# First product of the gated feed-forward in the second phase: second contraction chunk as bare integers, its scale in the silu, one bf16 term fewer

## The reference, cut to what matters

```
w1 = (fc1_q - 128) * fc1_scales[group of 128 rows]    # [256, 1024], two groups
w2 = (fc2_q - 128) * fc2_scales[group]                # [1024, 256]
h  = layernorm(x) * ln_gamma + ln_beta
y  = silu(h @ w1 + fc1_bias)
z  = y @ w2 + fc2_bias
out = x + tanh(g) * (x + 0.5 * z)                     # per token
```

## Time and profile before

| | |
|---|---|
| median of three executions | 1620.32 us (1616.96 to 1621.4) |
| span of the profiled execution, first to last instruction | 1614.4 us |
| median less that span | 5.9 us |
| PE busy in the span | 1486.5 us (92%) |
| DVE, ACT, POOL busy | 1316.4, 1135.2, 1034.7 us |
| second phase | from 611 us on |

### The profile page before, as it was taken

How to read it: one execution, slowest core, us unless ns; L and a number is a source line. 1 busy time by engine, 2 the same in 40 slices (tenths; PEclk the granted TensorE clock), 3 DMA queues, 4 the chain that set the end, 5 groups by cost and what they waited for, 6 DMA issues and landing times.

```text
span 1614.4 us, 42641 instructions
## 1 busy us (share of the span) xinstructions
PE 1486.5 (92%) x14155; PEld 1144.6 (71%) x14155; DVE 1316.4 (82%) x3187; ACT 1135.2 (70%) x2057; POOL 1034.7 (64%) x1392
## 2 busy tenths in 40 slices
PE   4999999999999972668999999999999999999997
PEld 2788888888888861435667676777777776777666
DVE  4698888888888875778988889898988889898742
ACT  7798888888888742355666666666666666676664
POOL 4588888888888744224556565665656566565445
PEclk9999999999999995588999999999999999999999
DMA  7322222322222002332223232232223232232200
GB/s 228 96 80 66 91 72 65 96 66 69 93 65 71 2 1 92 80 119 73 80 80 87 73 85 80 85 87 81 83 78 92 72 91 74 86 85 84 64 16 22
DMA packets 197690, 125.45 MB, mean 78 GB/s; under 512 B 44400, under 2 KB 196848, under 8 KB 197360
## 3 DMA queue, kind: packets, MB, share of 16 engines
q1 hardware_dynamic: 197616, 124.48, 26.2%
HBM read 92.69 MB, written 25.17 MB: 73 GB/s over the span
## 4 chain that ended last, share of the span: by engine, by line
PE 48%; SPq 4%; DVE 3%; issue 2%; DMA 2%; POOL 2%; ACT 1%; POOLq 0%
PE b_bank L1835 28%; PE b_bank L1910 7%; PE b_scoreT L1892 4%; PE b_score L1875 4%; PE b_bank L1843 2%; PE b_bank L1987 1%; SPq L1306 1%; DMA b_nmT<-b_nm 1%; DMA b_yT<-b_y 1%; SPq L1290 1%; DVE b_nm L1653 1%; SPq L1279 1%; PE b_bank L1925 1%; ACT b_E L1471 1%; SPq L1315 0%
## 5 line engine op out<-in xcount | busy, mean ns | idle before, releaser
L1471 ACT ACTIVATE b_E<-b_scoreT 128x1024 f32<-128x1024 f32 x256 | 262.2, 1024 | 152.5 <-PE b_scoreT L1892 151.3
L1653 DVE TENSOR_REDUCE b_nm<-b_score 128x4 bf16<-128x1024 f32 x256 | 313.3, 1224 | 54.6 <-PE b_score L1875 48.4
L31 ACT ACT_TABLE_LOAD x157 | 201.4, 1283 | 18.6 <-PEq L1059 15.2
L1835 PE MATMUL b_bank<-f,b_YT 128*128 128x256 bf16 x1536 | 190.3, 274 | 4.7 <-POOL b_YT L1404 4.6
L890 PE MATMUL bank<-hT,W1T 128*128 128x256 bf16 x1536 | 183.3, 273 | 2.4 <-DVE hT L706 1.7
L1835 PE MATMUL b_bank<-b_hT,f 128*128 128x256 bf16 x1536 | 183.4, 273 | 0.8 <-DVE X L1749 0.8
L890 PE MATMUL bank<-W2T,G 128*128 128x256 bf16 x1024 | 171.0, 272 | 6.7 <-DVE GT L780 6.2
L1835 PEld LDWEIGHTS b_bank<-f,b_YT 128*128 128x128 bf16 x1536 | 143.5, 98 | 39.7 <-issue 19.5
L1835 PEld LDWEIGHTS b_bank<-b_hT,f 128*128 128x128 bf16 x1536 | 147.7, 98 | 30.3 <-issue 12.6
L890 PEld LDWEIGHTS bank<-hT,W1T 128*128 128x128 bf16 x1536 | 148.0, 98 | 27.7 <-ACT G L549 4.0
L1388 POOL TENSOR_TENSOR b_v<-b_v,b_e 128x512 f32<-128x512 f32 x32 | 40.6, 1269 | 195.0 <-DVE b_e L1734 195.0
(11 more groups left out here) (222 smaller groups left out, 3524.8 us busy)
## 6 DMA issues: line engine op xcount, KB each, us to landing
b_Q<-q_dram SPq DMA_DIRECT2D x192, 64.0 KB, 2.6
b_K<-k_dram SPq DMA_DIRECT2D x192, 64.0 KB, 2.8
xin<-in_x SPq DMA_DIRECT2D x32, 256.0 KB, 3.2
ctxn<-in_ctx SPq DMA_DIRECT2D x32, 256.0 KB, 2.8
mask_in<-in_mask SPq DMA_DIRECT2D x32, 256.0 KB, 3.0
X<-in_x SPq DMA_DIRECT2D x32, 256.0 KB, 4.0
ctxt<-in_ctxT SPq DMA_DIRECT2D x32, 256.0 KB, 4.2
b_ctxt<-in_ctxT SPq DMA_DIRECT2D x32, 256.0 KB, 2.8
```

Source lines behind the costliest of these rows:

```text
L31: act.add_instruction(mybir.InstLoadActFuncSet(name=nc.get_next_instruction_name(), act_func_set_id=which, ins=[], outs=[]))
L1471: nc.scalar.activation(E[:, pair:pair + 2], scoreT_ps[:, :, :, :], ACT.Exp).then_inc(sig["E"], 1)
L1653: nc.vector.tensor_reduce(pair, score_ps[:, :, :, :], AX.X, ALU.max, negate=True).then_inc(sig["nm"], 1)
L1835: last = nc.tensor.matmul(out_tile, lhs(i, k), rhs(j, k), start=start and k == chunks[0] and (i, j) == TERMS[0], stop=stop and k == chunks ...
```

## The change

The second chunk of fc1 (input rows 128 to 255) is kept as the bare integers fc1_q - 128, which bf16 holds without a remainder, so the part (1, 0) of that chunk is all zero and its matmul is left out. The first chunk is scaled by s0 / s1 instead of s0, and the silu multiplies its input by s1, a [128, 1] operand per slice. gamma of the second chunk moves from the weights to hT, so mlp_high and mlp_low are two instructions each, one per chunk. The bias from beta is multiplied by s1 too. A test in the first phase finds out whether the integers and scales allow this; its result joins the mask flag, and the branch that PE takes then (`mask` true) keeps all three terms. The ratio s0 / s1 is computed in the first phase on DVE, written to DRAM and read back as a broadcast row.

```diff
@@ first phase, SP @@
+                                                          ("b1_raw", "fc1_bias_col"), ("s0_col", "fc1_s0_col"),
+                                                          ("s1_col", "fc1_s1_col"))]
+            + [(q1[:, :], a["fc1_q"][P:2 * P])]
...
+                if at_iteration(half, parity, NB):
+                    sp.wait_ge(sig["ratio"], 6)
+                    for i, src in enumerate((second["s0_col"], keep_s)):
+                        sp.dma_start(second["ratio"][i:i + 1].rearrange("o (h p) -> p (o h)", p=P), src[:, :],
+                                     allow_slow_non_contiguous=True).then_inc(sig["ratio_out"], 16)
+                if at_iteration(half, parity, NB + LAGS):
+                    sp.wait_ge(sig["ratio_out"], 32)
@@ first phase, DVE @@
+                if at_iteration(half, parity, 7):
+                    scale, first = second["s1_col"], second["s0_col"]
+                    nc.vector.tensor_tensor(zero_s[:, :], scale[:, :], scale[:, :], ALU.mult).then_inc(sig["square"], 1)
...
+                    nc.vector.tensor_tensor(first[:, :], first[:, :], inv_s[:, :], ALU.mult).then_inc(sig["ratio"], 1)
+                if at_iteration(half, parity, NB + 2):
+                    nc.vector.tensor_scalar(q1[:, :].bitcast(F32), q1[:, :], -128.0, None, ALU.add).then_inc(sig["exact"], 1)
+                    dve.wait_ge(sig["exact"], 1)
+                    nc.vector.tensor_reduce(second["exact"][:, 1:2], q1[:, :].bitcast(F32), AX.X, ALU.max,
+                                            apply_absolute_value=True).then_inc(sig["exact"], 1)
...
@@ setup_b, DVE @@
+            exact = second["exact"]
+            step(V_.tensor_tensor(exact[:, 0:1], exact[:, 0:1], exact[:, 1:2], ALU.min))
+            V_.tensor_tensor(peak[:, 1:2], peak[:, 1:2], exact[:, 0:1], ALU.min)
@@ phase_b, ACT @@
-                    nc.scalar.activation(hT[:, 0], whole_bank(BANK["hT"]), ACT.Copy).then_inc(sig["hhi"], 1)
+                    nc.scalar.activation(hT[:, 0, 0], bank[BANK["hT"]][:, 0], ACT.Copy)
+                    nc.scalar.activation(hT[:, 0, 1], bank[BANK["hT"]][:, 1], ACT.Copy,
+                                         scale=second["g_col"][:, 1:2]).then_inc(sig["hhi"], 1)
...
                         last = nc.scalar.activation(Y[:, 2 * j + i], bank[BANK[f"H{j}"]][:, i], ACT.Silu,
-                                                    bias=b1f[:, 2 * j + i:2 * j + i + 1])
+                                                    bias=b1f[:, 2 * j + i:2 * j + i + 1],
+                                                    scale=second["s1_col"][:, 2 * j + i:2 * j + i + 1])
@@ phase_b, DVE @@
-                    nc.vector.tensor_tensor(hT[:, 1], whole_bank(BANK["hT"]), hT[:, 0], ALU.subtract).then_inc(sig["hlo"], 1)
+                    nc.vector.tensor_tensor(hT[:, 1, 0], bank[BANK["hT"]][:, 0], hT[:, 0, 0], ALU.subtract)
+                    nc.vector.scalar_tensor_tensor(hT[:, 1, 1], bank[BANK["hT"]][:, 1], second["g_col"][:, 1:2], hT[:, 0, 1],
+                                                   ALU.mult, ALU.subtract).then_inc(sig["hlo"], 1)
@@ phase_b, PE @@
-            def product(out_tile, lhs, rhs, chunks, start=True, stop=True):
+            def product(out_tile, lhs, rhs, chunks, start=True, stop=True, last_terms=TERMS):
                 for k in chunks:
-                    for i, j in TERMS:
+                    terms = last_terms if k == chunks[-1] else TERMS
+                    for i, j in terms:
...
                         last = product(bank[BANK[f"H{j}"]][:, i], lambda s, k: f1[:, s, k, c * P:(c + 1) * P],
-                                       lambda s, k: hT[:, s, k], range(C))
+                                       lambda s, k: hT[:, s, k], range(C), last_terms=TERMS if mask else TERMS[:2])
```

More of the change, by code:

```diff
@@ L130, in build @@
             g_col=sb("g_col1", [P, C], F32), b_col=sb("b_col1", [P, C], F32), b1_raw=sb("b1_raw1", [P, HC], F32),
-            ones=sb("ones_row", [1, P], F32))
+            ones=sb("ones_row", [1, P], F32), s0_col=sb("s0_col", [P, HC], F32), s1_col=sb("s1_col", [P, HC], F32),
+            exact=sb("exact", [P, 2], F32),
+            ratio=nc.dram_tensor("ratio", (2, HID), F32, kind="Internal").ap())
         late = whole.enter_context(ExitStack())
@@ L846, in iteration @@
                         [P, C, P])).then_inc(sig["bv_rep"], 1)
+                if at_iteration(half, parity, 7):
+                    scale, first = second["s1_col"], second["s0_col"]
+                    nc.vector.tensor_tensor(zero_s[:, :], scale[:, :], scale[:, :], ALU.mult).then_inc(sig["square"], 1)
+                    dve.wait_ge(sig["square"], 1)
+                    nc.vector.tensor_scalar(zero_s[:, :], zero_s[:, :], 1e-36, None, ALU.is_le).then_inc(sig["ratio"], 1)
+                    dve.wait_ge(sig["ratio"], 1)
+                    nc.vector.tensor_scalar(keep_s[:, :], zero_s[:, :], -1.0, 1.0, ALU.mult, ALU.add).then_inc(sig["ratio"], 1)
+                    dve.wait_ge(sig["ratio"], 2)
+                    nc.vector.tensor_reduce(second["exact"][:, 0:1], keep_s[:, :], AX.X, ALU.min)
+                    nc.vector.tensor_tensor(inv_s[:, :], scale[:, :], zero_s[:, :], ALU.mult)
+                    nc.vector.tensor_tensor(scale[:, :], scale[:, :], keep_s[:, :], ALU.mult).then_inc(sig["ratio"], 1)
+                    dve.wait_ge(sig["ratio"], 3)
+                    nc.vector.tensor_tensor(keep_s[:, :], inv_s[:, :], keep_s[:, :], ALU.add)
+                    nc.vector.tensor_tensor(scale[:, :], scale[:, :], zero_s[:, :], ALU.add).then_inc(sig["ratio"], 1)
+                    dve.wait_ge(sig["ratio"], 4)
+                    nc.vector.reciprocal(inv_s[:, :], scale[:, :]).then_inc(sig["ratio"], 1)
+                    dve.wait_ge(sig["ratio"], 5)
+                    nc.vector.tensor_tensor(first[:, :], first[:, :], inv_s[:, :], ALU.mult).then_inc(sig["ratio"], 1)
[4 more added lines that the diff above has]
+                                            apply_absolute_value=True).then_inc(sig["exact"], 1)
+                    dve.wait_ge(sig["exact"], 2)
+                    nc.vector.tensor_scalar(second["exact"][:, 1:2], second["exact"][:, 1:2], 256.0, None,
+                                            ALU.is_le).then_inc(sig["exact"], 1)
                 for k in range(2):
@@ L1090, in _ @@
             step(V_.tensor_reduce(peak_all[:, 1:2], rows_ps[0:1, 1, 0:P], AX.X, ALU.min))
-            step(V_.tensor_scalar(any_masked[:, :], peak_all[:, 1:2], 0.0, None, ALU.is_equal))
+            step(V_.tensor_scalar(general[:, :], peak_all[:, 1:2], 0.0, None, ALU.is_equal))
             dve.wait_ge(s_pe, 2)
@@ L1237, in _ @@
         def _(sp):
+            ratio_row = second["ratio"].rearrange("(o g) h -> o (g h)", o=1)
             def load_weights(ints, layout, rows, scales, step):
@@ L1575, in iteration @@
                         last = nc.scalar.activation(f1[:, 0, c], whole_YT[:, c * HID:(c + 1) * HID], ACT.Copy,
-                                                    scale=second["g_col"][:, c:c + 1])
+                                                    scale=second["g_col"][:, c:c + 1] if c == 0 else 1.0)
                     last.then_inc(sig["f1hi"], 1)
@@ L1756, in iteration @@
                     dve.wait_ge(sig["b1_mm"], 1)
-                    nc.vector.tensor_tensor(b1f[:, :], second["b1_raw"][:, :], b1_ps, ALU.add).then_inc(sig["b1f"], 1)
+                    nc.vector.tensor_tensor(b1f[:, :], second["s1_col"][:, :], b1_ps, ALU.mult).then_inc(sig["b1s"], 1)
+                    dve.wait_ge(sig["b1s"], 1)
+                    nc.vector.tensor_tensor(b1f[:, :], b1f[:, :], second["b1_raw"][:, :], ALU.add).then_inc(sig["b1f"], 1)
                 if h:
@@ L1817, in iteration @@
                         last = nc.vector.scalar_tensor_tensor(f1[:, 1, c], whole_YT[:, c * HID:(c + 1) * HID],
-                                                              second["g_col"][:, c:c + 1], f1[:, 0, c], ALU.mult,
-                                                              ALU.subtract)
+                                                              second["g_col"][:, c:c + 1] if c == 0 else 1.0,
+                                                              f1[:, 0, c], ALU.mult, ALU.subtract)
                     last.then_inc(sig["f1lo"], 1)
@@ L2073, in iteration @@
                     first_bias()
-            some = pe.value_load(any_masked[0:1, 0:1], min_val=0, max_val=1)
+            some = pe.value_load(general[0:1, 0:1], min_val=0, max_val=1)
             with pe.If(some < 1):
```

26 lines of the change are left out of this document (16 added, 10 removed).

## The result

The changed kernel takes 1689.48 us (median of 4 runs, 1688.36 to 1695.16) where the kernel before takes 1619.34 in the same comparison: a ratio of 1.0444, with a 95% interval of 1.0424 to 1.0465. It is slower by some 70 us. The profiled execution took 1690.4 us, its span is 1688.6 against 1614.4, its mean granted clock 0.935 against 0.969.

What follows compares the result with a forecast made beforehand. The prediction took a ring through all engines in the second phase as the bound, PE a close second. Terms 40.8 + 2 - 1 - 4 = +38 us on the 1614.4 span, plus 5.9 for the median, gave 1658 us; range 1637 to 1690.

Steps and rivals of the forecast that it cites:

- The ring: Second phase: a dependency chain through all engines, 27.86 us per iteration, is the bound; PE's work at most 0.24 us shorter.
- The step that ends values_in 0.67 us earlier: Second phase: six matmuls left out in hidden(1) to hidden(3) end values_in, for which POOL waits, 0.67 us earlier.
- full collision: POOL's context_parts starts before DVE's hn, delaying hn and v: `on` +1.97 us, iteration +1.75 us; chance 0.45 at full clock.
- the rival with half a collision: hn's first instruction goes ahead of POOL's context_parts: +1.11 us per iteration, 1644 us in all; chance 0.20.
- the term of 40.8 us: Second phase: full collision's loss, taken as 1.70 us per iteration, times 24 steady iterations.
- the 4 us of early waits: Second phase: a few early iterations wait for something other than the ring; the longer ring covers these waits, -4 us.
- The silu's operand: ACT, second phase: the second [128, 1] operand costs 0.10 us per silu instruction, +0.20 us on the ring.
- The step that lets it decide who is first: With the silu's +0.20 us, hn is due too late and POOL's context_parts gets in first.
- at the full clock: The forecast of 1658 us assumed the full collision leaves PE's clock up; own range 1650 to 1668, chance 0.45.
- rival 4: Second phase: collision and a lower clock together, the clock put at 16 to 31 us, upper end 1690; chance 0.15.
- Once only: Ratio steps in first phase's iteration 7 and drain, and set-up steps: 0 to 5 us, taken as +2.
- The rival that PE is the bound: Second phase: matmuls left out save time directly, -28.7 us plus once-only 2, 1593 us; chance 0.09.

Runs made afterwards that it cites:

- run 2: Kernel before with only the third term of fc1's second chunk left out, nothing else of the change: 1672.25 us, ratio 1.0353.
- run 6: Changed kernel with POOL's split of the context made to wait for v, ahead of the bias rows: 1618.42 us, ratio 1.0014.
- run 5: Changed kernel with 14 extra matmuls, results overwritten, ahead of the hn transposes in PE's pause: 1660.82 us, ratio 1.0266.
- run 3: Changed kernel without the silu's scale operand: 1681.36 us, ratio 1.0400.
- run 1: Changed kernel with the third term of fc1's second chunk put back: 1641.07 us, ratio 1.0142.
- run 4: Changed kernel with the third term put back and without the silu's scale operand: 1627.4 us, ratio 1.0060.
- run 9: Changed kernel with v behind the fourth row of maxima and the ratio's steps in the first phase's drain: 1605.13 us, ratio 0.9921.
- run 10: Changed kernel with run 9's moves, and rs2 ahead of the first silu pair's split on POOL: 1606.31 us, ratio 0.9939.
- run 7: Changed kernel with DVE's two v instructions moved from behind hn to behind the fourth row of maxima: 1610.33 us, ratio 0.9941.
- run 8: Kernel before with only DVE's two v instructions moved behind the fourth row of maxima: 1616.23 us, ratio 0.9991.

## Why the prediction was right in its sign and wrong in its size

**The ring and the collision were right.** The step that ends values_in 0.67 us earlier measured 9.56 - 8.91 = 0.65. That context_parts then falls on hn and v is what runs 2, 6 and the timeline show. The forecast's full collision, +1.75 us an iteration, measured 29.67 - 27.86 = 1.81, with hn at 1.94 and v at 1.54 us a pair where near 2 and 1.5 were forecast; the rival with half a collision, +1.11, measured 29.05 - 27.86 = 1.19. I had treated them as alternatives, and both occur. So the term of 40.8 us measured 11 x 1.81 + 13 x 1.19 = 35.4 at the full clock. With the 4 us of early waits that the longer ring covers, forecast at 40.8 - 4 = 36.8, it is 31.4; run 5, with more of the longer kind, measures 33.7.

**The silu's operand was sized right,** 0.10 taken, 561 - 473 = 88 ns measured. The Trainium skill, page ScalarE: Activation LUTs, section What ACT_TABLE_LOAD costs, puts each such operand at about 93 ns; the trace agrees. The step that lets it decide who is first was right only in part: with the operand the longer collision ends 11 of 24 iterations, without it still 6 (run 3). That so small a delay can decide such an order is shown by runs 1 and 4, which differ by the operand alone, and by 14 us; there it is v that comes too late, not hn.

**The step that failed is the forecast's "at the full clock",** which left rival 4, collision and clock, with 0.15. From the earlier trace rows I read that a pause of 2.38 us leaves the clock up, and took that for the likelier case at 2.7. The runs show the clock at 1.2 GHz behind 19 of 24 pauses of 1.97 to 2.67 us, and at the full level behind others of the same length (1112.97 and 1142.64). One pause that left the clock up was no evidence for the next: in runs 9 and 10 the same single pause of 2.94 us was followed once by the lower level and once by the full one. What decides between equal pauses stays open. The price was 29.8 us over 24 iterations by run 5, which is most of what the forecast of 1658 lacks; rival 4 had put 16 to 31 for it.

**Once only** I took +2. The end of the set-up comes 615.01 - 610.76 = 4.3 us later, and iteration 7 alone cost 4.9: two of the [128, 8] steps took 0.62 and 0.66 us, not 0.2, beside POOL, and the pause behind them brought a half-clock stretch. For the end of the second phase I took -1; from the last of the 24 iterations on, the changed kernel needs 1688.6 - 1510.53 = 178.1 us, before 1614.4 - 1441.24 = 173.2, so +4.9. The same kind of stretches stand there (0.60 in the first 4 us, 0.82 to 0.84 from 1660.5 to 1670.5 us); I did not separate their part.

**The rival that PE is the bound** (1593 us) was wrong for this kernel and came partly true once v was off the ring: run 7 won 1618.69 - 1610.33 = 8.4 us in its comparison, not 27. Its 24 iterations take 662.04 us where those of run 8 take 675.00: 0.54 us an iteration, not the 0.90 of eight matmuls. About (6.1 - 1.1) / 22 = 0.23 of the difference are short waits of PE that run 8 hardly has (600 - 593.87 = 6.1 us in 22 iterations from 900 to 1500 us, against 1.1); the rest stays open. Another part of the shortfall lies ahead of these iterations, which begin at 776.38 us in run 7 and at 768.57 in the kernel before.

**The halves of mlp_high and mlp_low** at nothing: right by run 4.

## What to carry to other kernels

Taking work off an engine that waits anyway can do worse than fail to help: it moves the releases behind that work to an earlier time, and here one of them let another engine in first on a contended resource, in the middle of the chain that counts. Before removing work, list who is released by it and what that one then runs beside. Where such a chain and TensorE's stream are about equally long, shorten the chain first (here by moving v to a place where GpSimd is idle) and then remove matmuls; each alone gave nothing or a loss, both together 0.6 to 0.8%.

## What the runs showed of the hardware that I had not expected

- Pauses of about 2 us that recur in each iteration of 29 us were followed by stretches at 1.2 GHz in 19 of 24 iterations of the changed kernel (mean clock 0.95) and in fewer of run 2 (0.98 over 900 to 1500 us). Filling 1.7 us of each pause with matmuls whose results nobody reads held the clock at 1.00 over the 24 iterations and gave 29 us back.
- The pair of hn took 0.72 us with POOL idle and 1.94 beside POOL's split. That a DVE instruction in a two-port mode and a GpSimd instruction lock each other out for the whole instruction is what the Trainium skill's page SBUF — State Buffer, section Who interferes with whom, says. Runs 2 and 6 agree: hn takes 577 ns where the split comes early, 403 where it is made to wait. Who is first is not always to be read off the shown start times: xh in the earlier trace rows is shown 0.05 us ahead of POOL's instruction, and yet its first half takes 0.81 us where one of hn takes 0.40.
- Tiny DVE instructions may feel it as well: two [128, 8] TENSOR_SCALAR steps took 0.62 and 0.66 us while POOL was adding, the [128, 8] steps behind them, which are other operations, 0.16 to 0.20. No run moves these two alone.
